# Order of a fused scan-and-FFN kernel's dense work at the end of a chunk, and the place of the C-row broadcasts in SyncE's queue

## The reference

```python
h = layernorm(x) * (1 + ca) + sa
xs, z = split(h @ w_in.T + b_in); z = silu(z)
dt = softplus(xs @ w_dt.T + b_dt)
Bm, Cm = xs @ w_B.T + b_B, xs @ w_C.T + b_C          # 16 states
# per token: state = exp(A*dt)*state + dt*Bm*xs ; y = sum(state*Cm)
y = (y + D * xs) * z
x = x + ga * (layernorm(y @ w_out.T + b_out + h) * gamma + beta)
h = layernorm(x) * (1 + cb) + sb
s = h @ Win + bin                                    # 64 wide, "FFN input product"
g = sum_16(relu(s * W1 + b1) * W2) + b2
x = x + gb * (g @ Wout + bout)
```

## Time and profile before

| | |
|---|---|
| median of 3 runs | 4935.87 us (4935.53 to 4944.75) |
| the profiled execution | 4929.93 us, of it a span of 4928.2 us |
| granted TensorE clock, mean | 0.935 |
| TensorE / ScalarE / VectorE / GpSimd busy | 84% / 77% / 74% / 71% |
| steps with all stages | 30 of 34 |

### The profile page before, as it was taken

How to read it: one execution, slowest core, us unless ns; L and a number is a source line. 1 busy time by engine, 2 the same in 40 slices (tenths; PEclk the granted TensorE clock), 3 DMA queues, 4 the chain that set the end, 5 groups by cost and what they waited for, 6 DMA issues and landing times. The chain is left out here.

```text
span 4928.2 us, 58251 instructions
## 1 busy us (share of the span) xinstructions
PE 4129.9 (84%) x18432; PEld 2434.8 (49%) x18432; DVE 3630.0 (74%) x4620; ACT 3819.0 (77%) x6371; POOL 3516.3 (71%) x1775
## 2 busy tenths in 40 slices
PE   7888888888888888888888888888888888888877
PEld 3544545545455445455454554454554445544544
DVE  4877777777777777777777777777777777777775
ACT  4778778778787787787787777887877877778875
POOL 2777677776677776777777777767777767777674
PEclk8999999999999999999999999999999999999988
DMA  4666555665565665555765556655657555566554
GB/s 137 148 150 139 139 135 135 141 155 139 133 144 135 156 138 138 138 133 140 158 141 140 139 131 152 148 138 133 139 136 166 132 136 138 132 151 148 137 128 103
DMA packets 200747, 690.13 MB, mean 140 GB/s; under 512 B 25254, under 2 KB 25254, under 8 KB 147195
## 3 DMA queue, kind: packets, MB, share of 16 engines
q0 software_dynamic: 59904, 436.23, 43.3%
q1 hardware_dynamic: 140538, 250.19, 16.9%
HBM read 215.50 MB, written 34.63 MB: 51 GB/s over the span
## 5 line engine op out<-in xcount | busy, mean ns | idle before, releaser
L378 POOL TENSOR_TENSOR work<-work,c_bc 128x2048 f32<-128x2048 f32 x448 | 2040.8, 4555 | 737.2 <-DVE state L1169 476.5
L1161 DVE TENSOR_TENSOR_SCAN work<-work,state,b_ps 128x512 f32<-128x512 f32 x1792 | 2245.9, 1272 | 414.8 <-PE b_ps L493 403.5
L493 PEld LDWEIGHTS b_ps<-ident,work 128*128 128x128 f32 x8192 | 1022.0, 147 | 1328.3 <-issue 625.5
L493 PE MATMUL b_ps<-ident,work 128*128 128x128 f32 x8192 | 1307.5, 284 | 412.1 <-DVE work L1161 399.4
L876 ACT ACTIVATE work<-u_td,b_td 128x512 f32<-128x512 f32 x2048 | 1457.2, 712 | 122.6 <-PE b_ps L493 117.0
L866 ACT ACTIVATE work<-dt_t,neg_a 128x512 f32<-128x512 f32 x2048 | 1457.8, 712 | 84.7 <-DMA work<-work 83.7
L711 PE MATMUL dense<-h_t,w_in_t 128*128 128x512 f32 x1024 | 568.9, 657 | 7.4 <-DVE u_td L1244 7.3
L648 PE MATMUL dense<-h_t,w_in_t 128*128 128x512 f32 x1024 | 543.5, 643 | 3.8 <-ACT h_t L880 3.6
L619 PE MATMUL dense<-w_out_t,proj 128*128 128x512 f32 x1024 | 542.2, 630 | 0.0
L493 PE MATMUL dense<-ident,xn 128*128 128x128 f32 x1536 | 261.3, 298 | 325.5 <-POOL xn L442 208.3
L677 PE MATMUL dense<-xs_t,w_dt_t 128*128 128x512 f32 x1024 | 503.3, 595 | 0.0
(11 more groups left out here) (116 smaller groups left out, 4909.0 us busy)
## 6 DMA issues: line engine op xcount, KB each, us to landing
work<-work POOLq DMA_DIRECT2D x384, 1024.0 KB, 8.1
c_bc<-c_d SPq DMA_DIRECT2D x512, 256.0 KB, 3.4
xn<-in_x SPq DMA_DIRECT2D x128, 256.0 KB, 4.6
work<-xs_t POOLq DMA_DIRECT2D x32, 1024.0 KB, 7.7
x<-in_x SPq DMA_DIRECT2D x128, 256.0 KB, 4.5
out_dram<-x SPq DMA_DIRECT2D x128, 256.0 KB, 5.8
work<-in_wmod SPq DMA_DIRECT2D x2, 1024.0 KB, 6.6
w_in_t<-in_w_in_t SPq DMA_DIRECT2D x2, 1024.0 KB, 10.0
```

The costliest lines, as they stand in the source:

```text
L378: gp.tensor_tensor(out, states, c_of(s, n).rearrange("p (a t) -> p a t", a=1).to_broadcast([P, KD, T]), ALU.mult).then_inc(S["prod_done"], 1)
L493: return nc.tensor.transpose(dst, src, ident[:, :])
L1161: V.tensor_tensor_scan(ring[:, i % RING, :], ring[:, i % RING, :], b_ps[:, i % 2, :], state[:, i:i + 1] if s % NC else 0.0, ALU.mult, ALU. ...
```

## The change

Three things change; no instruction is added or removed.

1. SyncE issues spread_c in the last unit of each four (`i % KD == KD - 1`) and no longer in the first. The waits of the row stay: the product of row n-3.
2. In `ORDER` the FFN input product `s` comes ahead of `z.2` and `z.3`.
3. The u transposes move with the dense work: `ut.0` and `ut.1` into `z.2` (after its second and fourth matmul), `ut.2` and `ut.3` into `z.3` (after its first and third), so by 3, 3, 2 and 3 units later. Bank choices and the waits that guard banks follow.

```diff
-        z.2.0 ut.0 z.2.1 z.2.2 ut.1 z.2.3
-        s.0 ut.2 s.1 s.2 ut.3 s.3
-        z.3.0 z.3.1 z.3.2 z.3.3""".split()
+        s.0 s.1 s.2 s.3
+        z.2.0 z.2.1 ut.0 z.2.2 z.2.3 ut.1
+        z.3.0 ut.2 z.3.1 z.3.2 ut.3 z.3.3""".split()
...
-                    if i % KD == 0:
+                    if i % KD == KD - 1:
                         n = i // KD + 2
                         if n < N and has_s:
                             spread_c(s, n)
...
                     if m == 2:
-                        pe.wait_ge(S["bt_done"], at("bt_done", f, 1))
+                        pe.wait_ge(S["zmax_done"], at("zmax_done", s, 2))
                     if m == 3:
-                        pe.wait_ge(S["ut_done"], at("ut_done", f, 4))
-                        pe.wait_ge(S["zmax_done"], at("zmax_done", s, 3))
+                        pe.wait_ge(S["ut_done"], at("ut_done", f, 2))
+                        pe.wait_ge(S["s_copied"], at("s_copied", b, 1))
...
             def turn_u(s, f, tb):
-                to = inside(s, ("z.2", "z.2", "s", "s")[tb])
+                to = inside(s, ("z.2", "z.2", "z.3", "z.3")[tb])
                 if tb == 0:
                     pe.wait_ge(S["u_done"], at("u_done", f, KD))
-                    pe.wait_ge(S["zmax_done"], at("zmax_done", s, 2))
+                    pe.wait_ge(S["s_copied"], at("s_copied", s - 1, 1))
+                    pe.wait_ge(S["bt_done"], at("bt_done", f, 1))
                 if tb == 2:
                     pe.wait_ge(S["zmax_done"], at("zmax_done", s, 3))
-                    pe.wait_ge(S["bt_done"], at("bt_done", f, 1))
...
             def add_s(s, f, b, k):
                 if k == 0:
                     pe.wait_ge(S["h2_done"], at("h2_done", b, KD))
-                    pe.wait_ge(S["ut_done"], at("ut_done", f, 2))
-                    pe.wait_ge(S["zmax_done"], at("zmax_done", s, 2))
+                    pe.wait_ge(S["bt_done"], at("bt_done", f, 1))
...
             def add_g(s, c, k):
                 if k == 0:
                     pe.wait_ge(S["w2dg_done"], 1)
-                    pe.wait_ge(S["s_copied"], at("s_copied", c, 1))
+                    pe.wait_ge(S["ut_done"], at("ut_done", s, TB))
```

More of the change, by code:

```diff
@@ L47, in build_program @@
         z.1.0 z.1.1 bt.0 z.1.2 z.1.3
-        z.2.0 ut.0 z.2.1 z.2.2 ut.1 z.2.3
-        s.0 ut.2 s.1 s.2 ut.3 s.3
-        z.3.0 z.3.1 z.3.2 z.3.3""".split()
+        s.0 s.1 s.2 s.3
+        z.2.0 z.2.1 ut.0 z.2.2 z.2.3 ut.1
+        z.3.0 ut.2 z.3.1 z.3.2 ut.3 z.3.3""".split()
     LENGTH = dict(yz=0.6, xt=0.6, x2=0.6, ut=0.6, bt=0.5, res=0.5)
     GROUPS = ("g", "pre.0", "pre.1", "pre.2", "pre.3", "z.0", "xs.0", "xs.1", "xs.2", "xs.3", "dt.0", "dt.1", "dt.2",
-              "dt.3", "cb", "z.1", "z.2", "s", "z.3")
+              "dt.3", "cb", "z.1", "s", "z.2", "z.3")
     BEGIN, END = {}, {}
@@ L805, in dense @@
                         turn_b(s, f)
+                if has_b:
+                    for k in range(KD):
+                        yield slot("s", k)
+                        add_s(s, f, b, k)
                 for k in range(KD):
@@ L809, in dense @@
                         add_z(s, f, b, 2, k)
-                    if has_f and k in (0, 2):
+                    if has_f and k in (1, 3):
                         yield slot("ut", k // 2)
@@ L813, in dense @@
                 for k in range(KD):
-                    if has_b:
-                        yield slot("s", k)
-                        add_s(s, f, b, k)
+                    if has_s:
+                        yield slot("z", 3, k)
+                        add_z(s, f, b, 3, k)
                     if has_f and k in (0, 2):
@@ L819, in dense @@
                         turn_u(s, f, 2 + k // 2)
[L820 to L823, removed]
             def step(s, has_s, has_f, has_b, has_c):
@@ L1243, in take_u @@
                     dve.wait_ge(S["v_done"], at("v_done", s, (N - 1) * TB + tb + 1))
-                    V.tensor_copy(u_td[:, tb, :], inside(s, ("z.2", "z.2", "s", "s")[tb])[:, :]
+                    V.tensor_copy(u_td[:, tb, :], inside(s, ("z.2", "z.2", "z.3", "z.3")[tb])[:, :]
                                   ).then_inc(S["ut_done"], 1)
```

## The result

| | median us | runs | ratio to before, 95% interval |
|---|---|---|---|
| before | 4936.26 | 4 | |
| changed | 4508.35 (4503.84 to 4510.24) | 4 | 0.9128 [0.9112, 0.9144] |

The change takes 428 us off, 13.8 us for each of 31 steps. The prediction was 4520 us, and 13.5 us a step. The ratio is that of the means of the runs, here and in the table further down, so it differs a little from the ratio of the medians. The profiled execution took 4507.02 us, with a span of 4505.2 us and a mean granted clock of 0.985 (before: 0.935).

A forecast was written before the change was run, and what follows sets the result against it. No engine is full; engines stopping for each other in two loops bound the kernel. Gains of 8.5 + 5.0 = 13.5 us a step over 31 steps, 418 us, gave 4520 us; the range was 4400 to 4720 us.

The forecast's parts named there:

- Two loops: Engines stop for each other: for the x reload in a step's first third, and for u near its end.
- Part 1: Rows of C three units later free the x reloads one product earlier: 8.5 us a step, ends 6.0 and 9.5.
- The wait that stays for the fourth block: VectorE still waits about 1.2 us for GpSimd's line 421, which stands behind wide product 5.
- The clock at this place: Without the long TensorE stop near the fourth x block, matmuls and transposes run faster: some 2.0 us a step.
- The margin: First x reload lands near 2352.3, before GpSimd reaches line 416 at about 2353.8: 1.5 us to spare.
- Part 2: s ahead of z.2 and later u transposes fill TensorE's stop at step end: 5.0 us a step, ends 3.0 and 7.6.
- The cap by the chain's landing: Transposes into y_ps need the even chain of products landed, limiting the gain at the step's end to 7.6 us.
- The second relu: At the seam of the steps, ScalarE's second relu makes g of the next step wait 0.9 us.
- Only the queue: Rival: the later rows of C pay, the seam gives the u part back; 4672 us (4620 to 4720), chance 0.14.
- only the dense part: Rival: reloads of x stay late, only the reordered s and u transposes pay; 4781 us, chance 0.07.
- More than I think: Rival: TensorE never drops to 1.2 GHz at the two places, no chain limit; 4390 to 4440 us, chance 0.10.
- The slower rival: Next chunk's x load, waiting for the later fourth u transpose, lands too late for VectorE; about 4985 us, chance 0.06.

The follow-up runs named there:

- rows 4 to 7 alone: Kernel before with only rows 4 to 7 of C, those between which the stores and reloads of x stand, issued three units later: 4690.68 us.
- the experiment with the x block: Changed kernel with GpSimd adding the fourth block of x (line 421) one place earlier, ahead of wide product 5: 4497.97 us.
- the queue change alone: Kernel before with every row of C issued three units later and the dense order as before: 4689.29 us.
- the kernel with rows moved by one unit: Kernel before with every row of C issued one unit later instead of three: 4837.51 us.
- the dense change alone: Changed kernel with rows of C back in the first unit of each four; s ahead of z.2 and later u transposes stay: 4794.45 us.
- the relu experiment: Changed kernel with the first two relus of the FFN one unit earlier in ScalarE's queue: 4503.75 us.

## Why the prediction was right

**What bounds the kernel.** Two loops, one at each end of a step. Each experiment with one part alone removed one of them and left the other.

**Part 1, 8.5 us a step.** Measured 8.1. Its steps: the reloads come one product earlier (shown, and rows 4 to 7 alone do it). The wait that stays for the fourth block was said to be 1.2 us; it is 2.1 in the step shown of the changed kernel, whose line 421 ends at 2320.12,

```profile
2320.15 0.69 DVE L1177 BATCH_NORM_STATS2 norm<-x 128x6 f32<-128x512 f32 x1 [2.10 <-POOL x L421]
```

and the experiment with the x block shows that it comes from the place behind product 5. VectorE's wait for x fell by 6.8 us a step with the queue change alone, where 7.2 was said. The clock at this place was priced at 2.0 us a step; TensorE's busy time fell by 88 us, 2.8 us a step. The landings were read as fixed, 5.8 us for a store and 4.5 us for a reload. In the changed kernel they are

```profile
x<-in_x SPq DMA_DIRECT2D x128, 256.0 KB, 7.8
out_dram<-x SPq DMA_DIRECT2D x128, 256.0 KB, 4.2
```

in the median. For the first block in the step shown, the store issued at 2281.26 landed after 2.1 us and the reload after 7.9 us, so at 2291.25, and line 416 took it at 2292.87. The margin of 1.6 us, where 1.5 was said, came out by two errors of 3.7 and 3.4 us that cancel, which was luck. In the changed kernel it did no harm; in the kernel with rows moved by one unit the long landing did.

One term was missing. VectorE's small combination of statistics (L1174 before, L1173 now) took 157 ns in the mean; with the queue change alone it takes 772, in the changed kernel 729. Before, and with the queue change alone:

```profile
L1174 DVE SCALAR_TENSOR_TENSOR norm<-norm 128x4 f32<-128x4 f32 x64 | 10.0, 157 | 1.2 <-ACT norm L957 0.6 <-ACT norm L931 0.6
```

```profile
L1174 DVE SCALAR_TENSOR_TENSOR norm<-norm 128x4 f32<-128x4 f32 x64 | 49.4, 772 | 1.2 <-ACT norm L931 0.6 <-ACT norm L957 0.6
```

In the old order GpSimd ran nothing on data there: it issued a DMA and then waited for x. Now its line 416 runs at that moment (2292.87 for 1.57 us; the small operation begins at 2292.80 and takes 1.67). That is 39 us of VectorE's time with the queue change alone, 1.3 us a step. What of it the kernel pays is inside the measured 8.1.

**Part 2, 5.0 us a step.** Measured 4.7. The wait for u fell to 0.39 us in the step shown, where 1 was said. The cap by the chain's landing is real, but it is not what binds first: TensorE waits 2.1 us before z.3 for the second copy of u. The prediction names no such wait. The second relu, priced at 0.9 us, makes TensorE wait 0.95 us. My statement that a wait for the chain would appear was wrong for the changed kernel (ScalarE's wait for it is 72.4 us, before 83.7; that of y_ps is 1.6) and came true once the copy came earlier, with 24.5 us for y_ps and 58.7 us more for the decays. VectorE's wait for the u transposes was to fall under 80 us and is 103.8.

**The sum.** 13.5 us a step was said, 13.8 measured, but not quite for the reasons given: the parts alone give 12.9, and the rest, 0.9 us, is a term that the prediction did not have. That its total came out so near is in part luck: both parts were set a little too high, and this term fills the gap. The granted clock in three windows of one step of the kernel before (length, busy time and count by engine, then the clock, DMA share and GB/s):

```profile
2361.00:2370.00 9.00, 8.16 (x30) 4.53 (x30) 5.45 (x9) 7.47 (x14) 4.85 (x3) 0.81 0.53 143
...
2389.00:2396.00 7.00, 6.12 (x20) 3.52 (x21) 4.84 (x7) 6.89 (x12) 4.53 (x1) 0.69 0.75 153
...
2445.00:2460.00 15.00, 13.26 (x54) 7.97 (x54) 9.60 (x13) 7.01 (x13) 11.86 (x8) 0.79 0.75 158
```

The prediction counted the second and third dip. The first follows the 2.1 us stop for normalized x, which neither part touches. In the changed kernel there is no dip in the step shown:

```profile
2300.00:2312.00 12.00, 9.36 (x44) 5.40 (x42) 9.60 (x16) 10.67 (x19) 11.62 (x8) 1.00 0.79 202
2312.00:2322.00 10.00, 7.74 (x35) 4.28 (x34) 7.83 (x12) 9.02 (x18) 8.96 (x5) 1.00 0.68 150
```

The same stop is there (2.14 us), and the clock holds. Counted over 30 steps, the four matmul records behind this stop are slow (2.6 us or more, not 1.88) in 24 steps of the kernel before, in 11 with the queue change alone, in 15 with the dense change alone and in 3 of the changed kernel. So each part takes some of this dip away, 13 and 9 steps, and both 21: here the parts add up, and the missing 0.9 us isn't at this stop.

It shows when the clock is averaged over the whole step. One minus the granted clock, summed over a step (mean of 23 or 24 steps, in twenty equal slices from one gm copy to the next), is 8.5 us in the kernel before, 4.4 with the queue change alone, 6.4 with the dense change alone and 0.3 in the changed kernel. The parts take off 4.1 and 2.1 us, both 8.2: 2 us a step more than the sum. By the same slices, the dip that a single part leaves standing grows (at the end of the step from 3.5 to 3.8 us with the queue change alone, at the wait for x from 3.5 to 4.5 us with the dense change alone), and the dense change alone has a new one of 1.1 us, 7 to 15 us behind the gm copy, where the stop before z.3 lies. So the term is the clock's, as far as the rows show; why a dip grows when another goes, they don't.

**The rivals.** "Only the queue" and "only the dense part" gave 4672 and 4781 us; the whole came out at 4508, so neither happened, and the parts alone measured 4689 and 4794. "More than I think" was half true: the clock stayed up, but the copy of u bound the step's end before the cap did. TensorE's busy time of the kernel before was called a floor there; it is none, since it fell itself by 159 us. ScalarE's idle time in the last 50 us of a step, given as some 16 us, is 11.3 us (2410 to 2460); nothing in the sum hangs on it. The slower rival did not happen: VectorE waits for the x load nowhere but at the start.

## What to carry to other kernels

When a queue that only issues transfers makes a later transfer stand behind one that waits for a slow engine, look for a circle: here moving four row loads by three units was worth 8.1 us of 150 in each step. Move a stopped instruction behind independent work whose length you can count (5.6 us of matmuls against a stop of 6.6), and then name what lands next, for that caps the gain. When two stops go, look at the whole step's clock afterwards and not only at the two places, and look at durations too: a wait can be inside one.

## What the runs showed of the hardware

**A stop of 2.1 us does or does not cost TensorE its clock.** After the same stop, and the same work in the 14 us before it, four matmul records took 3.58 us in one kernel and 1.88 in another. Behind this stop TensorE was slow in 20 of 30 steps of the one kernel and in 3 of the other. In the relu experiment the lower clock was worth 54 us of TensorE's busy time against a wait of 31 us that had been removed. The Trainium skill, page "TensorE: Matmul & The Clock Gate", section "What's actually happening", says that the hardware looks at activity by free-running stretches, so that the point of a change depends on where in one the work lands. The rows fit that (same stop, another moment, another outcome), but none shows the stretches themselves.

**VectorE stands still for GpSimd inside an instruction.** A 128x4 operation with both inputs in SBUF took 2.18 us beside a wide product on GpSimd and ended with it to 0.02 us; where GpSimd ran nothing on data it took 0.16. Beside the short line 416 it took 1.67. The Trainium skill, page "SBUF — State Buffer", section "Who interferes with whom", says that a VectorE instruction with two SBUF inputs contends with a GpSimd instruction that reads SBUF. The rows agree, and the page of the profile does not list it as a wait.

**Landings are not constants.** With the same transfers in another order the median reload of a 256 KB block took 7.8 us instead of 4.5, and the median store 4.2 instead of 5.8.
